# A vision tower on one core: the convolution stage looks one plane ahead, and an attention unit is one map of two neighbouring key heads

## The reference, cut to what matters

```
# tokens: per channel a 31x31 correlation over the local standard deviation, then the mean over channels
result = dw_conv2d(image, (flat - mu) / (sd + 1e-9) / 961)
m1, m2 = box31(image) / 961, box31(image * image) / 961
h = mean_over_channels(result / (sqrt(m2 - m1 * m1) + 1e-9))         # nan -> 0
# attention: 256 tokens of 256; 16 query heads of 64, 8 key heads of 64, query heads 2h and 2h+1 use key head h
x = rmsnorm(h);  q = norm64(x @ Wq) * (q_gamma + 1) * 8;  k = norm64(x @ Wk) * (k_gamma + 1) * 8
sim = tanh(q k^T / 50) * 50 / 8, causal;  out_h = sum over its two query heads of softmax(sim) @ v_h
h = layernorm(h + out @ Wout)
h = layernorm(h + ffn(h))                                            # five ternary matrices, float32
```

## Time and profile before

| what | value |
|---|---|
| device time, median of 3 runs | 1977.88 us (1976.26 to 1985.11) |
| the profiled execution | 1977.19 us |
| its span, first to last instruction | 1975.5 us |
| PE busy | 1827.4 us, 93% of the span |
| DVE, ACT, POOL busy | 1122.4, 870.6, 399.7 us |
| token stage: first and last correlation matmul | 26.2 us, 552.4 us |
| attention stage, until its last projection | to about 1246 us |

### The profile page before, as it was taken

One profiled execution on the slowest core, in us unless ns is written; L12 is line 12 of the kernel. 1 busy time (PEld: TensorE's weight loads), 2 busy tenths in 40 slices (PEclk: granted clock), 3 DMA queues, 4 the chain that ended last, 5 costly groups with the idle time before them and its releaser, 6 DMA issues. The chain is left out here.

```text
span 1975.5 us, 31720 instructions
## 1 busy us (share of the span) xinstructions
PE 1827.4 (93%) x11768; PEld 1578.6 (80%) x11768; DVE 1122.4 (57%) x2084; ACT 870.6 (44%) x1073; POOL 399.7 (20%) x502
## 2 busy tenths in 40 slices
PE   5899999999969989999998998699999999999997
PEld 5788998988958877877887887587878787787876
DVE  8788888887866766675775674414142331414141
ACT  4654455556426764674775575122122222212221
POOL 2000000000111211121121112233332433333342
PEclk9999999999979999999999998799999999999999
DMA  5322222214011002000200100510000000000000
GB/s 170 109 78 86 87 79 108 94 54 142 23 37 61 23 16 81 23 16 18 86 24 8 66 23 16 236 44 22 0 23 1 22 23 1 22 0 22 1 11 12
DMA packets 17308, 97.10 MB, mean 49 GB/s; under 512 B 2937, under 2 KB 3065, under 8 KB 11650
## 3 DMA queue, kind: packets, MB, share of 16 engines
q1 hardware_dynamic: 17154, 94.96, 13.6%
HBM read 82.33 MB, written 24.15 MB: 54 GB/s over the span
## 5 line engine op out<-in xcount | busy, mean ns | idle before, releaser
L556 PE MATMUL conv<-w_hi,x_hi 128*128 128x368 f16 (+5 forms) x1320 | 355.1, 279 | 7.7 <-issue 5.7
L556 PE MATMUL conv<-w_lo,x_hi 128*128 128x368 f16 (+5 forms) x1320 | 356.0, 279 | 0.0
L556 PE MATMUL conv<-w_hi,x_lo 128*128 128x368 f16 (+5 forms) x1320 | 354.6, 279 | 0.0
L1322 ACT ACTIVATE raw_c<-ring,sh 128x512 f32<-128x512 f32 x128 | 88.1, 688 | 370.2 <-PE ring L1419 370.2
L1110 PE MATMUL mixed<-v,probs 128*128 128x65 f32 x1536 | 201.3, 282 | 22.6 <-DVE parts L990 19.3
L1419 PE MATMUL ring<-ha_hi,wh 128*128 128x512 f32 x512 | 207.8, 406 | 13.0 <-POOL ha_lo L1284 13.0
L1110 PEld LDWEIGHTS mixed<-v,probs 128*128 128x128 f32 x1536 | 185.6, 195 | 37.8 <-issue 22.8
L1284 POOL TENSOR_TENSOR ha_lo<-raw_c,ha_hi 128x512 fp32r<-128x512 f32 x128 | 164.9, 1288 | 210.1 <-DVE ha_hi L1334 210.1
L556 PEld LDWEIGHTS conv<-w_hi,x_hi 128*128 128x128 f16 x1320 | 192.8, 146 | 16.7 <-issue 8.4
L1419 PE MATMUL ring<-ha_lo,wh 128*128 128x512 f32 x512 | 205.4, 401 | 0.0
L1419 PE MATMUL ring<-hb_hi,wh 128*128 128x512 f32 x512 | 202.2, 395 | 0.0
(11 more groups left out here) (148 smaller groups left out, 3472.9 us busy)
## 6 DMA issues: line engine op xcount, KB each, us to landing
xt<-x_columns_in SPq DMA_DIRECT2D x12, 1163.0 KB, 5.6
xp<-x_patches_in SPq DMA_DIRECT2D x12, 1152.0 KB, 5.1
hidden_words<-hidden_weights_in SPq DMA_DIRECT2D x8, 1408.0 KB, 9.0
words<-hidden_words SPq DMA_DIRECT2D x32, 352.0 KB, 3.1
wh<-hidden_words SPq DMA_DIRECT2D x2, 4096.0 KB, 22.0
tokens<-planes SPq DMA_DIRECT2D x4, 1024.0 KB, 4.3
lines<-tokens SPq DMA_DIRECT2D x4, 1024.0 KB, 5.5
h<-tokens SPq DMA_DIRECT2D x4, 1024.0 KB, 6.8
```

Source lines behind the costliest of these rows:

```text
L556: ins = pe.matmul(out, xs[:, c, RI - 1 - i:RI - 1 - i + NR, :, x].rearrange("p r g -> p (r g)"), w, start=(t == 0), stop=(t == len(terms) ...
L1322: act.activation(raw[:, u % 4], bank, ACT.Gelu, scale=scale[:, m:m + 1]).then_inc(s_gelu, 1)
```

## The change

The token stage's bodies are written anew on every engine. Everything that belonged to plane n + 2 now belongs to n + 1, and the last part of plane n's deviation (`sum_across(n, 1)`, `variance`, `deviation`) is done at the beginning of body n. In the attention stage the queries' columns are permuted on the host so that the two maps of a unit belong to two neighbouring key heads. Keys are transposed once, `make` 11 and 15 and the buffer `keys` are gone, and two units instead of one share an output pair: the even one writes it, the odd one adds to it. An unused mask tile is dropped too.

```diff
@@ sync
             def first():
                 load_bands(1)
                 load_bands(2)
-                load_xt(0, 2, 2)
             def body(g, c, n, last):
                 if not (last and c >= 1):
+                    load_xt(*after(*after(g, c)), n + 2)
                     load_x(*after(*after(g, c)), n + 2)
-                if not last:
-                    load_xt(g + 1, c, n + CHANNELS)
@@ scalar
             def body(g, c, n, last):
-                split_hi((c + 1) % CHANNELS, n + 1)
-                square(n + 2)
-                turned(n + 1, 0)
-                turned(n + 1, 1)
-                mean_square(n + 1)
-                regroup(n + 2, 0)
-                regroup(n + 2, 1)
-                deviation(n + 1)
+                turned(n, 1)
+                mean_square(n)
+                split_hi((c + 1) % CHANNELS, n + 1)
+                square(n + 1)
+                deviation(n)
+                regroup(n + 1, 0)
+                regroup(n + 1, 1)
+                turned(n + 1, 0)
@@ vector
             def body(g, c, n, last):
+                sum_across(n, 1)
+                variance(n)
+                if more:
+                    sum_down(n + 1, 0)
+                    sum_down(n + 1, 1)
+                else:
+                    fold_weights()
                 dve.wait_ge(s_part, n * 4 + 4)
                 inverse(g, c, n)
-                if last and c == 2:
-                    fold_weights()
                 if more:
                     split_lo((c + 1) % CHANNELS, n + 1)
-                if more_down:
-                    sum_down(n + 2, 0)
-                scale(g, c, n, 0)
-                if more:
-                    sum_across(n + 1, 0)
-                if more_down:
-                    sum_down(n + 2, 1)
-                scale(g, c, n, 1)
-                if last and c == 2:
-                    scale_tokens()
+                for b in range(3):
+                    scale(g, c, n, b)
                 if more:
-                    sum_across(n + 1, 1)
-                    variance(n + 1)
-                scale(g, c, n, 2)
+                    sum_across(n + 1, 0)
+                else:
+                    scale_tokens()
                 scale(g, c, n, 3)
@@ tensor
             def first():
-                turn_sums(0, range(4))
-                correlate(0, 0, 0)
-                turn_sums(0, range(4, 8))
-                ...
+                turn_sums(0, range(8))
             def body(g, c, n, last):
-                correlate(c, n, 0)
-                turn_sums(n + 1, range(4))
-                correlate(c, n, 1)
-                turn_sums(n + 1, range(4, 8))
-                correlate(c, n, 2)
-                correlate(c, n, 3)
+                for b in range(3):
+                    correlate(c, n, b)
+                turn_sums(n + 1, range(4))
+                correlate(c, n, 3)
+                turn_sums(n + 1, range(4, 8))
@@ SLOTS
-    [("make", 11), ("make", 7), ("scale", 1)],
+    [("make", 7), ("scale", 1)],
     [("make", 12)],
-    [("make", 13), ("make", 14), ("make", 15)],
+    [("make", 13), ("make", 14)],
@@ attention, vector: scale
-                        dve.tensor_tensor(heads[:, 0:QH], heads[:, 0:QH], by[:, 0:QH].to_broadcast([P, QH, DH]), ALU.mult)
-                        for m in range(2):
-                            ins = dve.tensor_tensor(keys[:, tb, :, m], heads[:, QH:],
-                                                    by[:, QH:].to_broadcast([P, HEADS, DH]), ALU.mult)
-                        ins.then_inc(s_qn, 1)
+                        dve.tensor_tensor(heads, heads, by, ALU.mult).then_inc(s_qn, 1)
@@ attention, vector: emptying the keys' bank
-                        dve.tensor_tensor(kt[:, img % 2, 4 * r:4 * r + 4, P * tb:P * tb + P], bank, by,
-                                          ALU.mult).then_inc(s_emptied["keys"], 1)
+                        for m in range(2):
+                            by = gamma[:, m::2].rearrange("p (h t) -> p h t", t=1).to_broadcast([P, EB, P])
+                            ins = dve.tensor_tensor(kt[:, img % 2, m::2, P * tb:P * tb + P], bank, by, ALU.mult)
+                        ins.then_inc(s_emptied["keys"], 1)
@@ attention, vector: mix
+                        pair = o[:, img % 2, :, 2 * (hd // 2):2 * (hd // 2) + 2]
-                        dve.tensor_tensor(parts[:], got[:, :, :, 0:DH], rl[:].to_broadcast([P, 2, 2, DH]),
+                        dve.tensor_tensor(parts[:] if hd % 2 else pair, got[:, :, :, 0:DH], rl[:].to_broadcast([P, 2, 2, DH]),
                                           ALU.mult).then_inc(s_mixread, 1)
-                        dve.tensor_tensor(o[:, img % 2, :, hd], parts[:, :, 0], parts[:, :, 1],
-                                          ALU.add).then_inc(s_o, 1)
+                        if hd % 2:
+                            dve.tensor_tensor(pair, pair, parts[:], ALU.add).then_inc(s_o, 1)
```

More of the change, by code:

```diff
@@ L163, in token_stage, with planes @@
         LAST = GROUPS * CHANNELS - 1
-        def planes(eng, body, first, start=0):
+        def planes(eng, body, first):
             first()
-            with eng.Fori(start, GROUPS - 1) as g:
+            with eng.Fori(0, GROUPS - 1) as g:
                 for c in range(CHANNELS):
@@ L323, in first @@
                 regroup(0, 1)
[L324 to L327, removed]
                 act.wait_ge(s_tpad, 32)
-                deviation(0)
-                regroup(1, 1)
             def body(g, c, n, last):
-                if not (last and c == 2):
+                more = not (last and c == 2)
+                turned(n, 1)
+                mean_square(n)
+                if more:
                     split_hi((c + 1) % CHANNELS, n + 1)
-                if not (last and c >= 1):
-                    square(n + 2)
-                if not (last and c == 2):
-                    turned(n + 1, 0)
-                    turned(n + 1, 1)
-                    mean_square(n + 1)
-                if not (last and c >= 1):
-                    regroup(n + 2, 0)
-                    regroup(n + 2, 1)
-                if not (last and c == 2):
-                    deviation(n + 1)
+                    square(n + 1)
+                deviation(n)
+                if more:
+                    regroup(n + 1, 0)
+                    regroup(n + 1, 1)
+                    turned(n + 1, 0)
                 if last and c == 2:
@@ L560, in first @@
             def first():
-                turn_sums(0, range(4))
-                correlate(0, 0, 0)
-                turn_sums(0, range(4, 8))
-                correlate(0, 0, 1)
-                correlate(0, 0, 2)
-                turn_sums(1, range(4))
-                correlate(0, 0, 3)
-                turn_sums(1, range(4, 8))
-                for c in range(1, CHANNELS):
-                    body(0, c, c, False)
+                turn_sums(0, range(8))
             def body(g, c, n, last):
-                correlate(c, n, 0)
-                if not (last and c == 2):
+                more = not (last and c == 2)
+                for b in range(3):
+                    correlate(c, n, b)
+                if more:
                     turn_sums(n + 1, range(4))
-                correlate(c, n, 1)
-                if not (last and c == 2):
+                correlate(c, n, 3)
+                if more:
                     turn_sums(n + 1, range(4, 8))
-                correlate(c, n, 2)
-                correlate(c, n, 3)
-            planes(pe, body, first, 1)
+            planes(pe, body, first)
 BANKS = 3
@@ L610, in first_order @@
     order += [("make", 0, j) for j in (4, 5, 6)] + [("scale", 0, 0), ("sum", 0, 1), ("root", 0, 1)]
-    order += [("make", 0, j) for j in (3, 7, 8, 9, 10, 11)] + [("scale", 0, 1)]
-    return order + [("make", 0, j) for j in (12, 13, 14, 15)]
+    order += [("make", 0, j) for j in (3, 7, 8, 9, 10)] + [("scale", 0, 1)]
+    return order + [("make", 0, j) for j in (12, 13, 14)]
 def attention_order(last):
@@ L1090, in emit @@
                             pe.wait_ge(s_emptied["queries"], image(g, img) * 4 + 4)
-                            pe.wait_ge(s_emptied["keys"], image(g, img) * 4 + 4)
+                            pe.wait_ge(s_emptied["keys"], image(g, img) * 2 + 2)
                         pe.wait_ge(s_tanh, g * NH + n + 1)
```

41 lines of the change are left out of this document (14 added, 27 removed).

## The result

The changed kernel takes **1922.26 us** (median of 4 runs, 1919.14 to 1927.75), and the kernel before, run beside it, 1981.49 us (4 runs, 1976.26 to 1992.26). The ratio is 0.9686, with a 95% interval from 0.9651 to 0.972. The prediction said 1921, between 1907 and 1943.

A forecast was written before the change was run, and what follows sets the result against it. The prediction took the token stage to be paced by the DVE-ACT loop (43.6 us a plane against PE's 40.9) and attention by PE. 1977.2 - 37 (token stage) - 19 (attention) = 1921 us, range 1907 to 1943.

The forecast's parts named there:

- The token stage: Token stage: PE should go through without a wait, the stage ending near 514.6 instead of 552.4; -37 us, bounds -28 to -38.
- 12 planes of 40.9: Token stage on PE: 12 planes of 40.9 us, less 3.8 for two blocks the last plane lacks, 487.0 us.
- a scaling on DVE: Token stage before: 1.9 us of PE's waits were read as waiting for a scaling on DVE.
- the 10 us of slow clock: Token stage before: 10 us left over, put down to lower clock behind longer waits; most should go, 1 kept.
- Rival (A): Token stage: DVE still paces a little, 1 us a plane, 12 us come back, 1933 us; chance 0.14.
- Rival (D): Token stage: slower, PE's first transposes wait if `regroup` ends after 28.5, forecast at 21; chance with other losses 0.02.
- The border: Token stage's end: what follows the last plane's quarter 3 stays as before; 0, at most +2 us for `scale_tokens` waiting for POOL.
- The attention stage: Attention: fewer key transposes and shorter waits for DVE, against a new wait for `kt`; -19 us, bounds -28 and -9.
- waits before `mixed`: Attention: DVE is 0.7 us earlier, so under half of PE's 19.3 us of waits for `parts` goes; -8, between 0 and -13.
- first score waits for `kt`: Attention, each image's head: keys' bank is read twice on DVE, so the first score waits 0.3 us, 14 times; +4 us.
- The -14 of the transposes: Attention on PE: 256 transposes of keys become 128, 0.87 us per 8; -14 us.
- Rival (B): Attention gives nothing: PE's saved 14 us turn into waits for DVE's longer operations, 1940 us; chance 0.11.

The follow-up runs named there:

- e4: Changed kernel with all 12 planes of the token stage unrolled on TensorE, no loop there: 1918.61 us, ratio 0.9671 to the kernel before.
- e1: New token stage alone, with the attention stage of the kernel before: 1950.66 us, ratio 0.9851 to the kernel before.
- e5: Kernel before, still two planes ahead, one `sum_down` moved behind `variance` on DVE and one `regroup` behind `deviation` on ACT: 1960.03 us, ratio 0.9899.
- e2: New attention stage alone, with the token stage of the kernel before: 1955.78 us, ratio 0.9873 to the kernel before.
- e3: Changed kernel with PE's first group (three planes) written out ahead of the token stage's loop: 1921.85 us, ratio 0.9687 to the kernel before.
- e9: Changed kernel with each of a plane's four `regroup` operations done twice on ACT: 1927.35 us, ratio 0.9705 to the kernel before.
- e10: Changed kernel with all token-stage planes unrolled on TensorE and `make` 14 (keys) ahead of `make` 13 (queries): 1923.41 us, ratio 0.9685 to the kernel before.
- e7: Changed kernel with the 1536-column normalization on DVE split into 1024 columns of queries and 512 of keys: 1925.64 us, ratio 0.9698 to the kernel before.

## Why the prediction was right

**The token stage** (-37 forecast, -30.1 measured). PE goes through: no wait for `lines`, none for `down_m`. Counted from PE's start of quarter 0 at 235.93, with c = 2 of group 1, the steps came out as worked, by these timelines of PE, DVE and ACT:

```profile
235.93 0.26 PE L539 MATMUL conv<-w_hi,x_hi 128*128 128x217 f16 x1
...
264.37 1.92 PE L520 MATMUL turn<-ident,down_m 128*128 128x128 f32 x16
```

```profile
254.15 2.26 DVE L416 SCALAR_TENSOR_TENSOR std<-std,guess 128x2048 f32<-128x2048 f32 x1
...
260.86 2.55 DVE L431 TENSOR_TENSOR x_lo<-xp,x_hi 128x2304 f16<-128x2304 f32 x1
```

```profile
244.44 1.93 ACT L305 ACTIVATE std<-std 128x2048 f32<-128x2048 f32 x1 [0.31 <-DVE std L411]
...
252.84 3.90 ACT L286 ACTIVATE down_m<-down 128x1024 f32<-128x1024 f32 x4
```

| step | forecast | measured |
|---|---|---|
| `deviation` starts | 8.2 | 8.5 |
| DVE comes to `inverse` | 18.1 | 18.2 |
| `regroup` done | 21 | 20.8 |
| `x_lo` done | 27.3 | 27.5 |
| first block of transposes | 28.5 | 28.4 |
| one plane on PE | 40.9 | 40.86 (57.83 to 98.69) |

The first matmul was forecast at 27.6 and is at 27.62. The term that was mis-sized is "12 planes of 40.9", by 7.6 us: it left out what PE pays for going back to the head of its loop, because in the trace of before the one such gap is put down to DVE's `planes`. It is the 1.9 us that the prediction read as a wait for "a scaling on DVE". The timelines of PE and DVE before contradict that reading:

```profile
298.30 0.31 PE L556 MATMUL conv<-w_hi,x_hi 128*128 128x217 f16 x1 [1.95 <-DVE planes L453]
```

```profile
285.19 0.66 DVE L453 SCALAR_TENSOR_TENSOR planes<-conv,planes 128x512 f32<-128x512 f32 x1
...
297.15 0.67 DVE L453 SCALAR_TENSOR_TENSOR planes<-conv,planes 128x512 f32<-128x512 f32 x1
```

At 298.30 quarter 0 of plane 6 begins, which needs the scaling of quarter 0, done at 285.9. The one at 297.15 is of quarter 1, which begins only at 310.61. The kernel before had PE's first group written out ahead of the loop and so went back to its head once, at plane 6; the changed kernel goes back twice. With the loop gone, e4 ended the stage at 514.37 against the forecast 514.6, so the rest of the sum held to 0.2 us, and so did its choice that nearly all of the 10 us of slow clock would go.

Rival (A), that DVE paces at 1 us a plane, has no row for it: DVE waits for PE 14 times, and PE not once for DVE. Rival (D)'s decision point was wrong in a way that didn't matter. The prediction let the first block wait for both halves of `regroup` and so found 7.5 us of room; by the trace the first half is ready at 254.8 and used at 264.4, 9.6 us, and the second has some 18.

**The border** (0 to +2 forecast, +1.8 in the wait). From the last correlation to the next stage's first matmul PE stands for 5.15 us, where it stood 3.36. The timeline of DVE shows why:

```profile
519.16 2.15 DVE L449 TENSOR_TENSOR planes<-planes 128x512 f32<-128x512 f32 x1
521.35 0.69 DVE L452 TENSOR_TENSOR planes<-planes,valid 128x512 f32<-128x512 f32 x1
521.96 2.18 DVE L471 TENSOR_SCALAR lines<-lines,rms 128x256 f32<-128x256 f32 x8
524.06 0.68 DVE L443 SCALAR_TENSOR_TENSOR planes<-conv,planes 128x512 f32<-128x512 f32 x1
```

`scale_tokens` itself takes 2.2 us instead of the 8.6 of the earlier trace rows, since POOL's last operation on `wqkv_lo` had ended (at 520.8); but it begins only when quarter 3 of PE is done and stands ahead of its scaling. What was late was the work ahead of it: the operation at 519.16 has two SBUF inputs and took 2.15 us beside POOL, where the same takes 0.69 elsewhere. The +2 stands, then, but it fell on another operation than the prediction said: on the scalings and not on `scale_tokens`. e1, with the old attention stage, has the same 5.2 us, and e5, with the old order of the scalings, 3.4. With the rule of the Trainium skill that the prediction named ("SBUF — State Buffer", section on two separate sides) the trace agrees: the operation ends at 521.3, 0.5 us after POOL's.

**The attention stage** (-19 forecast). By the traces it is -20.1 between the scores and -2.0 in the first image (first transposes of `lines`, at 527.37, to the first score: 33.5 us against 35.5; forecast -1 besides its share of the transposes), and +1.1 at the end, which was not followed up. The terms:

| term | forecast | measured |
|---|---|---|
| waits before `mixed` | -8 | 22.6 to 14.5, -8.1 |
| of these, left for `parts` and `o` on DVE | 11 | 13.9 (before 19.3) |
| first score waits for `kt` | +4 | +1.8 (2.8 in 7 waits, 0.2 each in the loop; before 1.0 in one) |
| `raw` in one operation of 1536 | 1.8 us | 1.79 us |
| `o` of 256 columns | 0.45 us | 0.44 us |

The sum of the waits was right and its split off by 3 us: DVE's part fell by 5.4 and not by 8, and POOL's `probs` lost 2.9 us of waits, which the prediction hadn't counted. That the two make -8 is luck. Other waits of PE in the stage moved too, which the prediction left out: for DVE's `o` from 2.3 to 3.8, for ACT's `ot` from 4.9 to 6.0, and for the normalized rows from 7.7 to 6.8. The -14 of the transposes cannot be seen by itself in one row. With the measured waits, -14 - 8.1 + 1.8 + 1.5 + 1.1 - 0.9 gives -18.6, and the stage shows -21.0 in all (-20.1 - 2.0 + 1.1), so it can be off by some 2 us, clock included. Rival (B) is out by e2.

**The total.** Against the profiled execution before, the forecast was -56, and the profiled one after has -49.4. The median has -59.2 beside its own before. The stage sum misses 6.9 us of token stage, and gets some back since the trace that the prediction was made on has the shortest of the three old attention stages seen. That 1921 and 1922.26 lie so near is in part luck.

## What to carry to other kernels

Where two engines hand a chain back and forth, look first for what the waiting engine could do in the wait: moving one 5 us piece of work behind the hand-over (with `deviation` moved ahead of one `regroup` on ACT) gave 24.8 of the 31.4 us here, and looking one plane ahead without the cover gained nothing. For the room of a step that moves, read which part of its result each wait asks for; a deadline taken for the whole was 2 to 10 us too strict. Where a small gap comes back at the period of a loop, suspect the loop first, whatever the profile names as its releaser, and check whether the named release is the one that the wait asks for; count the returns before and after an edit that shortens the written-out start.

## What the runs showed of the hardware that was not expected

- A return to the head of the loop on PE in the token stage comes with a gap of 1.7 to 2.3 us in each trace: 2.29 and 1.92 in the changed kernel, 2.12 and 1.89 in e1, 2.05 in e3, 1.71 and 2.10 in e9, 1.65 in e2, none in e4 and e10, which have no loop there. Behind it the clock is granted at about half for some 3 to 5 us (0.77 and 0.56 in the windows), which costs about 1.7 more: 30.1 us from there to the first block of transposes (152.59 to 182.72), against 28.4 in a plane without the gap (235.93 to 264.37); behind the second it is 30.2 (278.83 to 308.98).
- The same wait of 1.28 us in the last image is followed by 2.4 GHz in one execution and by 40 us of 1.2 GHz in another. From this wait to the feed-forward stage's first matmul are 57.3 us in the one (1154.26 to 1211.54) and 71.0 in the other (e7, 1149.74 to 1220.69), so it is worth 13.7 us here.
